# Building a graph's count matrix with ranges of 5 to 13 nodes instead of 25, and spreading the first mean's products

## The chip, the cores and the metric

The kernel runs on 1 core of one Trainium2 chip. The metric is the device time of one execution in microseconds (us), median of the runs shown. An engine works through its own queue in order: TensorE (PE, with its weight loads as PEld), VectorE (DVE), ScalarE (ACT), GpSimd (POOL) and SyncE (SP), which only issues DMAs here. They meet at counting semaphores.

## The reference

Four graph layers, each behind a layer norm and a ReLU, with a residual, on 3125 nodes of 256 features and 50000 edges. `dst` is sorted, and its density falls with the node number as 1/sqrt, so the first nodes have many more edges than the last.

```python
dst = jnp.minimum((3125 * jax.random.uniform(...) ** 2.0).astype(jnp.int32), 99999)   # then sorted
...
edge_index = jnp.stack([src, dst])
h = jnp.maximum(_layernorm(x, axis=-1), 0.0)
x = x + _L0_gnn_ref(h, edge_index, ...)   # hypergraph convolution, twice: mean over dst, then over src
h = jnp.maximum(_layernorm(x, axis=-1), 0.0)
x = x + _L1_gnn_ref(h, ..., src, dst, edge_type_16)      # messages summed by dst, then a GRU cell
h = jnp.maximum(_layernorm(x, axis=-1), 0.0)
x = x + _L2_gnn_ref(h, edge_index, ...)   # GCN
h = jnp.maximum(_layernorm(x, axis=-1), 0.0)
x = x + _L3_gnn_ref(h, edge_index, ...)   # attention
```

## The kernel before

The 3125 nodes are 25 tiles of 125. The kernel first turns the edge list into a dense matrix of edge counts, `adj` (source node by destination node, fp8), with TensorE, in the stage `build`. All layers after it (`main`, from 390 us on) multiply with that matrix. The change lies in `build`, and in two waits of `main`.

In `build` the destination nodes are cut into 125 windows of 25 nodes. A window gets as many **slots** of 128 edges as its expected number of edges asks for, plus a margin: 551 slots in all, from 38 for the first window to 3 for the last. For each slot VectorE writes three one-hot matrices of 128 edges: `hot_lo` (source within its tile, 128 wide, L1516) and `hot_rel` (relation, and destination, L1518), both for eight slots at once in `bulk`, and `hot_keys` (destination within the window times source tile, 625 bytes written as 314 16-bit words, L1528), one instruction for each slot, four to a `quad`. TensorE multiplies them (`window`: L1699 twice per slot, 325 and 300 columns in two PSUM banks, and L1701 once, 25 columns, for the relation counts `CT`). When a window is complete, ScalarE copies both banks into `adj` (`evict`, L1622), and after the fifth window of a tile also `CT` (L1626).

While a tile's windows are built, the product of the tile before it is done: the first mean over `dst`, 25 matmuls of 512 columns (`agg`, L1673), in pieces of 5, 7, 7 and 6 behind the tile's windows. The product of the last tile stands alone at the end. Behind a product come, in turn, `scale_high` on ScalarE (L1632), `combine` on VectorE (L1541), `split` on ScalarE (L1639) and the low half on GpSimd (L1434). The in-degree of a tile is a one-column matmul (`in_degree`, L1680) from `CT`; VectorE reads it in `inverse_degree` (L1534 to L1536).

`hot_lo` and `hot_rel` have two buffers of eight slots: `bulk(m)` waits until TensorE has used the slots of bulk m - 2. `hot_keys` has three buffers of four.

Nothing is scheduled by a planner: the queues are as the code writes them. VectorE's (`vector`) runs through the quads, with the other work put between them: statistics of x after quads 3, 6 and 10, the other groups' keys after quad 8, and `inverse_degree(b - 1)` and `combine(b - 2)` where the last slot of tile b lies.

Ahead of the slots stands a setup chain: a search for the edge number at which each window starts. The last edge of each of 400 chunks is loaded, VectorE counts (L1442), GpSimd gathers one row of 125 for each window (L1417), VectorE counts again, TensorE spreads the windows' starts over the slots (L1713), and GpSimd gathers the edges of all slots in five groups of 128 slots (L1399). Keys are computed (L1463 to L1470), turned by TensorE (L1708), and halved (L1506 to L1510).

Of the kernel before, what the change touches and what calls it, by code (L numbers as in the profile page):

```python
# [24 lines left out]
P = 125  # L25
# [17 lines left out]


def capacities():


    out = []
    for n in range(WINDOWS):
        share = math.sqrt((n + 1) / WINDOWS) - math.sqrt(n / WINDOWS)  # L50
        mean = EDGES * share
        out.append(math.ceil((mean + 5 * math.sqrt(mean * (1 - share))) / SLOT))
    return out


CAP = capacities()
FIRST = [sum(CAP[:n]) for n in range(WINDOWS + 1)]
SLOTS = FIRST[WINDOWS]
GROUPS = -(-SLOTS // SLOT)
PADDED = EDGES + (max(CAP) + 1) * SLOT  # L60
# [66 lines left out]
class Kernel:  # L127


    def __init__(self, nc, ctx, d):  # L130
# [269 lines left out]
def main(k, built):  # L400
# [220 lines left out]
    def tensor(pe):  # L621

        def flip(f):
            i, n = divmod(f, NF)
            if f == 0:
                pe.wait_ge(built["evicted"], WINDOWS)
# [18 lines left out]
        def back1(p):  # L645
# [682 lines left out]
def build(k):  # L1328
# [18 lines left out]
    hot, used, evicted, ct_out = (k.sem("build_" + n) for n in ("hot", "used", "evicted", "ct_out"))  # L1347
    deg_in, deg_out, acc, aw_out, t_ready, hi, lo = (k.sem("build_" + n) for n in ("deg_in", "deg_out", "acc", "aw", "t", "hi", "lo"))

    temp = k.adj_all[:, :, :].rearrange("p t c -> p (t c)").bitcast(F32)  # L1350
    SG = SLOT * GROUPS

    def area(n, width):
        return temp[:, n * SG:n * SG + width]

    raw = temp[:, 0:3 * SG].bitcast(I32).rearrange("p (g e k) -> p g e k", g=GROUPS, k=3)
    raw_rows = temp[:, 0:3 * SG].bitcast(I32).rearrange("p (g n) -> p g n", g=GROUPS)
    tile, lo_key, rel_key, din, hi_key = (area(3 + n, SG).rearrange("p (g e) -> p g e", e=SLOT) for n in range(5))
    win_of, chosen, mark = area(8, SG), area(9, SG), area(10, SG)
    ends, near = area(11, CHUNKS).bitcast(I32), area(12, P).bitcast(I32)  # L1360
    col = area(13, 64)
    pidx, thresh, count, count_i, near_count, before, at2 = (col[:, n:n + 1] for n in (0, 1, 2, 3, 4, 5, 6))
    rhs = col[:, 8:10]
    slot_at, slot_f, slot_i = col[:, 10:10 + GROUPS], col[:, 20:20 + GROUPS], col[:, 30:30 + GROUPS].bitcast(I32)
    where = col[:, 40:40 + 2 * GROUPS].rearrange("p (g k) -> p g k", k=2)
# [1496 lines left out]
```

## Time and profile before

| | |
|---|---|
| median of 3 runs | 1432.39 us (1431.55 to 1432.98) |
| profiled execution | 1432.54 us, its span 1430.5 us |
| PE busy | 1306.7 us (91%), 9866 matmuls |
| DVE busy | 837.4 us (59%) |
| ACT, POOL busy | 437.8 us, 180.2 us |
| `build` | from 0 to 390 us of the span |

Times of rows are microseconds from the span's start, or ns for the mean of one. A matmul's or VectorE instruction's duration overlaps with its neighbour's, so that the rate is read from the distance of the starts.

### The profile page before, as it was taken

How to read it: one execution, taken by the hardware profiler on the slowest of the kernel's cores; microseconds unless marked ns; L12 is line 12 of the kernel's file. 1: busy time of each engine (PE TensorE's matmuls, PEld its weight loads, DVE VectorE, ACT ScalarE, POOL GpSimd, SP SyncE). 2: the span in 40 equal slices, each digit the busy share in tenths (PEclk: the TensorE clock that was granted, in tenths of full speed). 3: DMA queues.
4: the chain of work that ended last, by engine and by line, in shares of the span. 5: the costliest groups of instructions: out<-in, count | busy, mean ns of one | idle time of the engine just before them, and what ended most of it. 6: DMA issues, size and time to landing. Idle time of an engine off the chain costs nothing.

```text
span 1430.5 us, 24598 instructions
## 1 busy us (share of the span) xinstructions
PE 1306.7 (91%) x9866; PEld 1009.1 (71%) x9866; DVE 837.4 (59%) x2257; ACT 437.8 (31%) x971; POOL 180.2 (13%) x321
## 2 busy tenths in 40 slices
PE   2669999999999999999999999999999998999940
PEld 1436666666689999766688888767777777888830
DVE  6999998888545556533335544244535364444566
ACT  3322343444487666211111122122222222222200
POOL 3340000000110000000001111000001011111153
PEclk9779999999999999999999999999999999999975
DMA  5000000000041111200024442011111011111124
GB/s 175 38 20 1 1 1 1 1 1 1 1 158 47 59 47 59 81 1 0 1 82 151 144 157 94 26 34 34 34 34 44 24 34 38 37 36 38 38 62 130
DMA packets 44264, 70.30 MB, mean 49 GB/s; under 512 B 6696, under 2 KB 28551, under 8 KB 44145
## 3 DMA queue, kind: packets, MB, share of 16 engines
q1 hardware_dynamic: 36428, 53.67, 11.2%
q10 hardware_dynamic: 4132, 10.63, 2.2%
q0 software_dynamic: 3584, 4.38, 1.1%
q8 instruction: 79, 1.29, 0.4%
q14 instruction: 41, 0.33, 0.1%
HBM read 38.78 MB, written 29.85 MB: 48 GB/s over the span
## 4 chain that ended last, share of the span: by engine, by line
PE 81%; DVE 12%; POOL 2%; ACT 2%; DMA 1%; issue 1%; POOLq 0%; DVEq 0%; ACTq 0%
PE ps L395 35%; PE ps L675 9%; PE ps L1673 9%; PE ps L1699 7%; PE ps L642 3%; PE ps L736 3%; PE ps L738 3%; DVE big L1528 3%; PE ps L631 2%; POOL adj L618 2%; PE ps L779 2%; PE ps L762 2%; DVE whh L1528 1%; PE ps L742 1%; PE ps L740 1%
## 5 line engine op out<-in xcount | busy, mean ns | idle before, releaser
L395 PE MATMUL ps<-big,pairB 125*128 125x250 fp8e4 (+1 forms) x2600 | 302.9, 267 | 0.6 <-DVE big L1068 0.6
L395 PEld LDWEIGHTS ps<-big,pairB 125*128 125x128 f16 x2600 | 238.8, 98 | 30.0 <-issue 2.8
L590 POOL TENSOR_TENSOR st<-st,mhalf 125x1 f32<-125x1 f32 x100 | 59.3, 593 | 879.0 <-DVE st L1145 879.0
L1622 ACT ACTIVATE adj<-ps 125x325 fp8e4<-125x325 f32 x250 | 99.9, 455 | 199.0 <-PE ps L1701 198.8
L1673 PE MATMUL ps<-pairA,adj 125*125 125x512 f16 x625 | 154.2, 385 | 0.0
L395 PE MATMUL ps<-adj,pairB 125*128 125x250 fp8e4 (+1 forms) x1300 | 146.0, 267 | 1.8 <-DVE pairB L1203 1.8
L395 PE MATMUL ps<-adj,pairA 125*128 125x250 fp8e4 (+1 forms) x1300 | 139.2, 267 | 0.0
L395 PEld LDWEIGHTS ps<-adj,pairB 125*128 125x128 f16 x1300 | 123.2, 98 | 20.0 <-DVE pairB L1203 2.0
L675 PE MATMUL ps<-pairA,adj 125*125 125x512 f16 x625 | 135.2, 379 | 0.0
L395 PEld LDWEIGHTS ps<-adj,pairA 125*128 125x128 f16 x1300 | 120.9, 98 | 19.3 <-issue 7.7
L675 PEld LDWEIGHTS ps<-pairA,adj 125*125 125x125 fp8e4 x625 | 85.7, 137 | 48.9
L1528 DVE TENSOR_SCALAR big<-big 128x314 uint16<-128x314 f16 x368 | 114.8, 381 | 0.0
L1673 PEld LDWEIGHTS ps<-pairA,adj 125*125 125x125 fp8e4 x625 | 77.8, 137 | 36.7
L1701 PE MATMUL ps<-wih 128*128 128x25 bf16 x551 | 98.2, 178 | 0.0
L1174 DVE TENSOR_TENSOR big<-ps,gates_b 125x512 f32<-125x512 f32 x25 | 17.2, 688 | 117.8 <-PE ps L742 117.8
L1068 DVE CAST big<-ps 125x500 fp8e4<-125x500 f32 (+1 forms) x87 | 53.8, 625 | 51.4 <-PE ps L631 51.1
L1699 PE MATMUL ps<-big,W 128*128 128x325 fp8e4 x376 | 67.7, 310 | 14.9 <-DVE big L1528 14.7
L885 ACT ACTIVATE whh<-adj 125x1625 fp8e4<-125x1625 fp8e4 (+1 forms) x50 | 75.1, 1501 | 0.1
L1701 PEld LDWEIGHTS ps<-wih 128*128 128x128 bf16 x551 | 56.2, 102 | 26.4
L1699 PE MATMUL ps<-big,Wg 128*128 128x325 fp8e4 x360 | 63.1, 303 | 4.4 <-DVE big L1528 4.3
L631 PE MATMUL ps<-identb,adj 125*125 125x125 bf16 x625 | 63.3, 222 | 3.4 <-ACT big L878 3.3
L1528 DVE TENSOR_SCALAR whh<-big 128x314 uint16<-128x314 f16 x184 | 60.4, 393 | 4.0 <-PE ps L1701 4.0
(239 smaller groups left out, 1772.8 us busy)
## 6 DMA issues: line engine op xcount, KB each, us to landing
t_adjTp<-big SPq DMA_DIRECT2D x25, 400.0 KB, 2.3
big<-t_adjTp ACTq DMA_DIRECT2D x25, 400.0 KB, 3.9
t_xh<-work SPq DMA_DIRECT2D x13, 256.0 KB
t_z<-big SPq DMA_DIRECT2D x25, 128.9 KB
pairB<-in_x SPq DMA_DIRECT2D x5, 640.0 KB, 11.6
t_h0p<-pairB SPq DMA_DIRECT2D x5, 640.0 KB
work<-t_xh SPq DMA_DIRECT2D x25, 128.0 KB, 2.3
xin<-t_xh SPq DMA_DIRECT2D x25, 128.0 KB, 2.3
```

The costliest lines, as they stand in the source:

```text
L395: last = pe.matmul(out, src[:, j, FEAT * part + 128 * c:FEAT * part + 128 * (c + 1)], rhs(j, p), start=(j + part == 0 and not begun), stop ...
L590: g.tensor_tensor(st[:, 9:10], st[:, 8:9], k.mhalf[:, 0:1], ALU.pow).then_inc(S[rstd], 1)
L631: last = pe.matmul(k.ps[0:P, f % 4, (j - j0) * P:(j - j0 + 1) * P], k.adj[:, i, PITCH * j:PITCH * j + P], k.identb[:, 0:P], start=True, st ...
L642: last = pe.matmul(k.ps[0:P, 6 + i % 2, 0:FEAT], stationary(i // 2 % 2, i, c), w[:, c, :], start=(c == 0), stop=(c == KC - 1))
L675: last = pe.matmul(k.ps[0:P, i % 4, :], k.adj[:, j, PITCH * i:PITCH * i + P], k.pairA[:, j, :], start=(j == 0), stop=(j == TILES - 1))
L885: s.activation(junk[:, 0:(j1 - j0) * P].rearrange("p (j c) -> p j c", c=P), cols[:, i, j0:j1, 0:P], ACT.Copy, saturate=False, accum_out=(k ...
L1068: v.tensor_copy(slots[:, i % 4, j0:j1, 0:P], k.ps[0:P, f % 4, 0:(j1 - j0) * P].rearrange("p (j c) -> p j c", c=P), saturate=False).then_in ...
L1528: last = v.tensor_scalar(k.hot_keys[q % 3][:, u, 0:HALVES * 2].bitcast(U16), k.iota_keys[:, 0:HALVES], k.key_half[:, s:s + 1], k.key_byte[ ...
L1622: last = s.activation(out[:, :, d0:d1], k.ps[0:P, 2 * (n % 2) + a, 0:(d1 - d0) * TILES] .rearrange("p (n j) -> p j n", j=TILES), ACT.Copy, ...
L1673: last = pe.matmul(k.ps[0:P, 6 + i % 2, :], k.adj[:, j, PITCH * i:PITCH * i + P], k.pairA[:, j, :], start=(j == 0), stop=(j == TILES - 1))
L1699: pe.matmul(k.ps[0:128, bank + a, 0:(d1 - d0) * TILES], low, keys[:, d0 * TILES:d1 * TILES], start=start, stop=True, skip_group_check=True)
L1701: pe.matmul(k.ps[0:128, 4 + b % 2, WIN * q:WIN * (q + 1)], rel[:, 0:128], rel[:, 128:128 + WIN], start=start, stop=True, skip_group_check= ...
```

## The change

- The windows are narrower, and their width differs from tile to tile (5 to 13 nodes, `tile_windows`): 405 windows and 606 slots. By tile, from the first: 102, 49, 40, 32, 28, 25, 25, 21, 20, three of 21, three of 18, four of 16, five of 14, and 13 slots. A slot is one key matmul of 125 to 325 columns and one relation matmul of 5 to 13 columns; L1528's successor writes 63 to 163 words.
- Neighbouring windows of a tile share a PSUM bank up to 20 nodes (197 **blocks**), and four banks are in turn. ScalarE empties a block at a time.
- `hot_keys` has a ring of 32 slots and no wait of its own; `hot_lo` and `hot_rel` keep two buffers of eight. `bulk` now writes the keys too.
- The 25 matmuls of a tile's product are given out slot by slot by a list, `SUMMED`: in even steps over the slots from number 104, but not before five slots after the tile's last. Evaluated, the list spreads the product of tile 0 over slots 107 to 124; all 25 of each product of tiles 1 to 21 stand behind one slot, the fifth after the tile's last (156, 196, 228, 256, 281, 306, 327, 347, 368, 389, 410, 428, 446, 464, 480, 496, 512, 528, 542, 556, 570).
- ScalarE reads the in-degree (`degree`); VectorE's `inverse_degree(t)` comes after the bulk with slot END[t] - 2, and `combine(t)` after the bulk with slot END[t] + 14, where END[t] is the slot behind which the product of tile t ends.
- The setup searches each slot's window directly: GpSimd writes a table of the first node of each slot's window with 36 runs, each an iota for the node and most a second for the slots to skip; TensorE turns it into columns; five gathers of chunk rows take the place of one.
- `main` waits for all 25 low halves ahead of its first product, where it waited for 22 and then for each of the last.

In VectorE's queue, one tile late in the build (`W`, `Wg` are `hot_lo`, `wih` is `hot_rel`, `big` and `whh` hold `hot_keys`). Before:

```order
L1516 TENSOR_TENSOR W<-big,work 128x1024 [waits build_used]
L1518 TENSOR_TENSOR wih<-big,work 128x8x2x25
L1528 TENSOR_SCALAR whh<-big 128x314 [waits build_used]
L1528 TENSOR_SCALAR whh<-big 128x314 x3
L1534 COPY indeg<-ps 125x1 [waits build_deg_in]
L1535 TENSOR_SCALAR rsB<-ps 125x1
L1536 RECIPROCAL rsB<-rsB 125x1 [waits build_ok]
L1541 SCALAR_TENSOR_TENSOR work<-ps,rsB,work 125x256 [waits build_lo,build_aw]
L1528 TENSOR_SCALAR big<-big 128x314 [waits build_used]
L1528 TENSOR_SCALAR big<-big 128x314 x3
```

And now, the bulks of slots 464 to 471 and 472 to 479 and what follows them (slot 474 is the last of tile 15):

```order
L1607 TENSOR_TENSOR W<-big,work 128x1024 [waits build_used]
L1609 TENSOR_TENSOR wih<-big,work 128x8x2x16
L1618 TENSOR_SCALAR whh<-big 128x100 x8
L1607 TENSOR_TENSOR Wg<-big,work 128x1024 [waits build_used]
L1609 TENSOR_TENSOR wih<-big,work 128x8x2x16
L1618 TENSOR_SCALAR whh<-big 128x100 x2
L1618 TENSOR_SCALAR whh<-big 128x63
L1618 TENSOR_SCALAR whh<-big 128x100 x5
L1633 SCALAR_TENSOR_TENSOR work<-ps,rsB,work 125x256 [waits build_lo,build_aw]
L1626 TENSOR_SCALAR rsB<-indeg 125x1 [waits build_deg_out]
L1627 RECIPROCAL rsB<-rsB 125x1 [waits build_ok]
L1607 TENSOR_TENSOR W<-big,work 128x1024 [waits build_used]
```

Before, the degree read here was that of a tile whose slots had been past for a tile; now it is that of the tile whose last slot is five slots back, and it stands ahead of the next bulk. In TensorE's queue late in the build, before:

```order
L1680 MATMUL ps<-ones,CT 125x1 [waits build_ct_out]
L1673 MATMUL ps<-pairA,adj 125x512 [waits build_t,build_evicted]
L1673 MATMUL ps<-pairA,adj 125x512 x4
L1699 MATMUL ps<-big,W 128x325 [waits build_hot,build_evicted]
L1699 MATMUL ps<-big,W 128x300
L1701 MATMUL ps<-wih 128x25
```

And now, at slots 511 and 512:

```order
L1767 MATMUL ps<-ones,CT 125x1 [waits build_ct_out]
L1783 MATMUL ps<-whh,Wg 128x200 [waits build_evicted]
L1785 MATMUL ps<-wih 128x8
L1783 MATMUL ps<-big,W 128x200 [waits build_hot]
L1785 MATMUL ps<-wih 128x8
L1760 MATMUL ps<-pairA,adj 125x512 [waits build_t]
L1760 MATMUL ps<-pairA,adj 125x512 x24
L1783 MATMUL ps<-big,W 128x200 [waits build_evicted]
```

The one-column matmul of the degree now stands just ahead of a slot that waits for VectorE (`build_hot`), and the product is in one piece behind that slot. In GpSimd's queue, from the first gather on, before:

```order
L1417 DMA adj<-in_dst_rows,adj 125x125 [waits build_first]
L1389 IOTA big 128x640
L1420 MEMSET ones 128x125
L1394 TENSOR_TENSOR work<-work,mhalf 125x5 [waits build_var]
L1396 TENSOR_TENSOR work<-work 125x5 [waits build_rstd]
L1399 DMA adj<-in_edges,adj 128x384 [waits build_indexed]
L1399 DMA adj<-in_edges,adj 128x384 x4
```

And now:

```order
L1467 DMA adj<-in_dst_rows,adj 128x125 [waits build_chunk]
L1451 TENSOR_TENSOR work<-work,mhalf 125x5 [waits build_var]
L1453 TENSOR_TENSOR work<-work 125x5 [waits build_rstd]
L1467 DMA adj<-in_dst_rows,adj 128x125 [waits build_chunk] x2
L1472 DMA adj<-in_edges,adj 128x384 [waits build_indexed]
L1467 DMA adj<-in_dst_rows,adj 128x125 [waits build_chunk] x2
L1472 DMA adj<-in_edges,adj 128x384 [waits build_indexed] x4
```

Three more instructions and a wait (`build_var`) stand between the first row gather and the first gather of edges; ahead of it stand 56 iotas instead of 16. The core of the diff:

```diff
+def tile_windows(tile):
+    best = None
+    for width in range(5, WIDEST + 1):
+        cuts = [(a, min(a + width, P)) for a in range(0, P, width)]
+        need = [slots_for(P * tile + a, P * tile + b) for a, b in cuts]
+        cost = sum(n * (33 + b - a) for n, (a, b) in zip(need, cuts))
+        if best is None or cost < best[0]:
+            best = cost, cuts, need
+    return best[1:]
...
+    cost = [33 + WINDOWS[w].width for w in SLOT_WINDOW]
+    total, past, done, out = sum(cost[SUM_FROM:]), 0, 0, []
+    for s in range(SLOTS):
+        if s >= SUM_FROM:
+            past += cost[s]
+            ready = TILES * sum(stop + 5 <= s for stop in STOP)
+            done = max(done, min(ready, round((TILES - 1) * TILES * past / total)))
+        out.append(done)
...
@@ main, tensor
-                if p == 0 and c == 0 and (j == 0 or j >= EARLY):
-                    pe.wait_ge(built["lo"], max(j + 1, EARLY))
+                if p == 0 and u == 0:
+                    pe.wait_ge(built["lo"], TILES)
@@ build, vector
-        def quad(q):
-            if q >= 3:
-                dve.wait_ge(used, QUAD * (q - 2))
-            for u in range(QUAD):
-                s = QUAD * q + u
-                last = v.tensor_scalar(k.hot_keys[q % 3][:, u, 0:HALVES * 2].bitcast(U16), k.iota_keys[:, 0:HALVES],
+            for u in range(BULK):
+                s = BULK * m + u
+                if s >= SLOTS:
+                    break
+                n = (TILES * WINDOWS[SLOT_WINDOW[s]].width + 1) // 2
+                last = v.tensor_scalar(k.hot_keys[m % RING][:, u, 0:2 * n].bitcast(U16), k.iota_keys[:, 0:n],
                                        k.key_half[:, s:s + 1], k.key_byte[:, s:s + 1], ALU.is_equal, ALU.mult)
+                if u % QUAD == QUAD - 1 or s == SLOTS - 1:
+                    last.then_inc(hot, 1)
...
+            for t in range(TILES):
+                if (END[t] - 2) // BULK == m:
+                    inverse_degree(t)
+                if (END[t] + 14) // BULK == m:
+                    combine(t)
@@ build, scalar
+            act.wait_ge(used, blk.stop)
+            s.activation(k.adj[:, :, PITCH * i + blk.at:PITCH * i + blk.at + blk.width], k.ps[0:P, n % 4, 0:blk.width * TILES]
+                         .rearrange("p (n j) -> p j n", j=TILES), ACT.Copy, scale=1.0 / CNT, saturate=False).then_inc(evicted, 1)
...
+        for m in range(SLOTS + 64):
+            while counted < TILES and STOP[counted] + 6 <= m:
+                degree(counted)
...
+            while n < len(BLOCKS) and BLOCKS[n].stop <= m:
+                evict(n)
...
+            while halved < TILES and END[halved] + 16 <= m and halved < scaled:
+                split(halved)
...
+            while scaled < TILES and END[scaled] + 2 <= m:
+                scale_high(scaled)
@@ build, tensor
+        for s in range(SLOTS):
+            if STOP[counted] + 4 == s:
+                in_degree(counted)
+                counted += 1
...
+            slot(s)
+            while done < SUMMED[s]:
+                t, j = divmod(done, TILES)
+                agg(t, j, j + 1)
+                done += 1
```

## Rows read from the trace of the kernel before

**Rows 1.** The page: TensorE's granted clock in 40 slices of the span.
```profile
PEclk9779999999999999999999999999999999999975
```
**Rows 2.** Timeline of the setup (start, duration, engine, line, what, idle before).
```profile
1.76 2.85 POOL L1389 IOTA adj<- 128x38 f32 x12
...
7.56 1.36 POOL L1417 DMA_INDIRECT adj<-in_dst_rows,adj  x1 [2.73 <-DVE adj L1555]
...
9.68 1.74 DVE L1448 BATCH_NORM_STATS2 work<-pairB 125x6 f32<-125x256 f32 x5 [1.07 <-DMA pairB<-in_x]
...
12.26 1.21 POOL L1394 TENSOR_TENSOR work<-work,mhalf 125x5 f32<-125x5 f32 x1 [2.47 <-DVE work L1454]
...
14.69 0.15 DVE L1562 COPY adj<-adj 125x1 f32<-125x1 f32 x1 [2.52 <-DMA adj<-in_dst_rows,adj]
...
18.96 1.24 POOL L1399 DMA_INDIRECT adj<-in_edges,adj  x1 [5.22 <-DVE adj L1571]
...
24.51 0.24 DVE L1463 CAST adj<-adj 128x128 f32<-128x128 int32 x1
...
28.53 0.23 DVE L1506 TENSOR_SCALAR big<-work 128x128 f32<-128x128 f32 x1 [1.89 <-ACT work L1615]
...
29.90 1.23 DVE L1516 TENSOR_TENSOR W<-big,work 128x1024 bf16<-128x1024 f16 x1
```
**Rows 3.** DMA issues, 0 to 60 us: KB each, us from issue to landing.
```profile
adj<-in_edges,adj POOLq DMA_INDIRECT x5, 3.8
```
**Rows 4.** Timeline of VectorE, one bulk of eight slots and the next.
```profile
87.79 1.21 DVE L1516 TENSOR_TENSOR Wg<-big,work 128x1024 bf16<-128x1024 f16 x1
88.92 0.57 DVE L1518 TENSOR_TENSOR wih<-big,work 128x400 bf16<-128x400 f16 x1
89.41 2.26 DVE L1528 TENSOR_SCALAR big<-big 128x314 uint16<-128x314 f16 x8
91.58 1.22 DVE L1516 TENSOR_TENSOR W<-big,work 128x1024 bf16<-128x1024 f16 x1
```
**Rows 5.** Groups of VectorE by form (busy us, mean ns | idle before).
```profile
L1557 DVE TENSOR_SCALAR adj<-adj 125x640 f32<-125x640 f32 x1 | 0.5, 544 | 0.0
L1467 DVE TENSOR_SCALAR adj<-adj 128x512 f32<-128x512 f32 x1 | 0.4, 427 | 0.0
L1467 DVE TENSOR_SCALAR adj<-adj 128x128 f32<-128x128 f32 x1 | 0.2, 227 | 0.0
```
**Rows 6.** Timeline of TensorE, two slots at the full clock.
```profile
92.08 0.43 PE L1699 MATMUL ps<-big,Wg 128*128 128x325 fp8e4 x2
92.34 0.17 PE L1701 MATMUL ps<-wih 128*128 128x25 bf16 x1
92.37 0.43 PE L1699 MATMUL ps<-big,Wg 128*128 128x325 fp8e4 x2
```
**Rows 7.** Timeline of TensorE: end of tile 0's product, and the last ones.
```profile
120.40 1.49 PE L1673 MATMUL ps<-pairA,adj 125*125 125x512 f16 x6
...
365.51 1.29 PE L1673 MATMUL ps<-pairA,adj 125*125 125x512 f16 x5
...
375.87 1.29 PE L1673 MATMUL ps<-pairA,adj 125*125 125x512 f16 x5
...
384.46 5.61 PE L1673 MATMUL ps<-pairA,adj 125*125 125x512 f16 x25
```
**Rows 8.** Timeline: an eviction of ScalarE, and what follows the last product.
```profile
287.32 0.75 ACT L1622 ACTIVATE adj<-ps 125x325 fp8e4<-125x325 f32 x2 [1.35 <-PE ps L1701]
...
390.11 0.47 ACT L1632 ACTIVATE work<-ps,rsB 125x256 f32<-125x256 f32 x1 [4.41 <-PE ps L1673]
...
390.62 0.48 DVE L1541 SCALAR_TENSOR_TENSOR work<-ps,rsB,work 125x256 f32<-125x256 f32 x1 [5.03 <-ACT work L1632]
```
**Rows 9.** Busy time by stretch: PE, PEld, DVE, ACT, POOL, granted clock, DMA, GB/s.
```profile
48.00:50.00 2.00, 0.01 (x1) 0.00 (x0) 1.93 (x13) 0.00 (x0) 1.05 (x1) 1.00 0.79 328
50.00:52.00 2.00, 1.99 (x12) 1.19 (x12) 2.00 (x4) 0.00 (x0) 1.55 (x2) 0.56 0.00 0
```

More of the change, by code:

```diff
@@ L42 @@
 BATCH = 5
[L45 to L52, printed above, removed]
-    return out
[L56 to L60, printed above, removed]
+ORDER = tuple(range(TILES))
+Window = namedtuple("Window", "turn at width slots slot block")
@@ new lines, with summing @@
+WINDOWS, BLOCKS, RUNS = plan()
+SLOTS = sum(w.slots for w in WINDOWS)
+SLOT_WINDOW = [n for n, w in enumerate(WINDOWS) for _ in range(w.slots)]
+GROUPS = -(-SLOTS // SLOT)
+RUN_SPLIT = next(r[0] for r in RUNS if r[0] >= SLOT)
+PADDED = EDGES + (max(w.slots for w in WINDOWS) + 1) * SLOT
+def summing():
+    cost = [33 + WINDOWS[w].width for w in SLOT_WINDOW]
[6 more added lines that the diff above has]
+        out.append(done)
+    return out
@@ L1357, in build @@
[L1357 to L1363, printed above, removed]
@@ L1364, in build, with part_row @@
-    slot_at, slot_f, slot_i = col[:, 10:10 + GROUPS], col[:, 20:20 + GROUPS], col[:, 30:30 + GROUPS].bitcast(I32)
-    where = col[:, 40:40 + 2 * GROUPS].rearrange("p (g k) -> p g k", k=2)
+    def part_row(row, count, at, width):
+        return k.adj_all[:, row:row + count, SPARE + 4 * at:SPARE + 4 * (at + width)].bitcast(F32)
+    raw_rows = part_row(0, GROUPS, 0, 3 * SLOT).bitcast(I32)
+    raw = raw_rows.rearrange("p g (e k) -> p g e k", k=3)
+    tile, lo_key, rel_key = (part_row(5, GROUPS, SLOT * n, SLOT) for n in range(3))
@@ new lines, in build @@
+    din, hi_key = (part_row(10, GROUPS, SLOT * n, SLOT) for n in range(2))
+    ends = part_row(15, 1, 0, CHUNKS).rearrange("p o c -> p (o c)").bitcast(I32)
+    near = part_row(16, GROUPS, 0, P).bitcast(I32)
+    mark = part_row(16, GROUPS, P + 3, CHUNKS // 2).bitcast(F16)
+    col = part_row(22, 1, 0, 128).rearrange("p o c -> p (o c)")
+    pidx = col[:, 0:1]
+    where = col[:, 10:10 + 2 * GROUPS].rearrange("p (g k) -> p g k", k=2)
+    count, near_count, slot_f = (col[:, 20 + 10 * n:20 + 10 * n + GROUPS] for n in range(3))
@@ L1423, in gpsimd @@
-        for n in range(GROUPS):
+        table(RUN_SPLIT, SLOTS)
+        iota(k.iota_keys, [[1, KWI]], 0, 0)
+        g.memset(k.ho_all[:, :], 0.0).then_inc(iotas, 1)
+        gather_near(0)
+        root(0)
+        gather_near(1)
+        gather_near(2)
+        gather(0)
+        for n in range(3, GROUPS):
+            gather_near(n)
+        for n in range(1, GROUPS):
             gather(n)
@@ new lines, in inverse_degree, with combine @@
+        def inverse_degree(t):
+            i = ORDER[t]
+            dve.wait_ge(deg_out, t + 1)
+            own.link(v.tensor_scalar(k.rsB[:, i:i + 1], k.indeg[:, i:i + 1], 1.0, 1.0 / CNT, ALU.max, ALU.mult))
+            v.reciprocal(k.rsB[:, i:i + 1], k.rsB[:, i:i + 1]).then_inc(known, 1)
+        def combine(t):
+            i = ORDER[t]
+            dve.wait_ge(aw_out, t + 1)
+            wait_past(dve, lo, t - 1)
+            stt(out=k.t[t % 2], in0=k.ps[0:P, 6 + t % 2, FEAT:2 * FEAT], scalar=k.rsB[:, i:i + 1], in1=k.aw[t % 2],
@@ L1572, in vector @@
+        starts(0, 1)
+        moments_of(0)
+        keys(0, 1)
+        starts(1, GROUPS)
         magnitudes()
```

377 lines of the change are left out of this document (193 added, 184 removed).

## The prediction

> **What bounds the kernel now.** I read the clock and the busy shares by slices first: after the first twelfth of the span TensorE is busy and at its full clock throughout [rows 1], so nothing later than the build can hide or give anything. The build is the only stage changed. Its timelines show three parts. Until 29.90 us a chain over all engines finds the edges of the slots; the first bulk of one-hot matrices starts there [rows 2]. From there to tile 0's product, which ends at 120.40 + 1.49 = 121.9, VectorE never rests: eight slots cost it 91.58 - 87.79 = 3.79 us [rows 4], and TensorE only about 0.29 us a slot [rows 6], 2.3 us for eight. From then on TensorE sets the pace: a late tile takes 375.87 - 365.51 = 10.36 us [rows 7], which is 15 slots of 0.29 (4.4) and 25 products in 5.61 [rows 7]. The last product ends at 390.1. What follows is the same in both kernels, so I forecast the place of that end. The new wait for all low halves in the main stage costs nothing: the last low half follows its product by about 2.5 us (two of its steps take 1 us, [rows 8]), and in both kernels 14 groups of transposes stand between.
>
> **The new prices.** TensorE: eight VectorE-made slots showed 92.37 - 92.08 = 0.29 us for 650 columns; 650 columns at 2.4 GHz are 0.27, so a slot of 26 x width columns costs (26 x width)/2400 + 0.02: 0.10 for width 7, 0.11 for 8. VectorE: `hot_lo` keeps 88.92 - 87.79 = 1.13 us for eight slots; `hot_rel` goes from 400 to 256 elements, 0.49 to 0.33. A key instruction of 314 words took 2.17/8 = 0.27 [rows 4]. Its size now falls to 63 to 163 words, and the trace has no such size. The 640-wide one took 544 ns, and 384 elements more cost 427 - 227 = 200 ns without a column operand [rows 5]: 1.95 elements per ns. Taking size off, the 640-wide one has 544 - 328 = 216 ns left, and the key instruction, whose duration is 2.26 - 7 x 0.272 = 0.358 us [rows 4], has 358 - 161 = 197: nearly the same fixed part, so I take two elements a cycle for it too, and for the distance of two of them 0.272 - 0.161, 0.11 us, + words/1950. The bounds are this and all of it fixed (0.27). Width 7 gives 0.154, width 8 0.160, so a slot costs VectorE 0.18 + 0.16 = 0.34 us instead of 0.47.
>
> The Trainium skill ("VectorE: DVE Perf Modes", the perf-mode tier table) has `tensor_scalar` on 16-bit data in SBUF at four elements a cycle, not two. By that rule the 314-wide instruction is 0.19 fixed and 0.08 by size, and the narrow ones would be 0.05 to 0.06 dearer than I take. The equal fixed parts above speak for two; what four would give is a rival below.
>
> **Setup.** GpSimd has 53 table iotas where 12 took 2.85 us [rows 2]: between 0.11 (the short ones lie that close) and 0.24 each, 6 to 13 us, so the first row gather issues at 9 to 15 instead of 7.56. Its rows landed at 14.69, 7.1 us on, while the loads of x filled the queues; the edge gathers needed 3.8 [rows 3]. I take 15. Then, one behind another: count and start of group 0, 1.3 (16.3); the statistics of x, 9.68 to 12.26, 2.6 (18.9); `root`, 1.4 (20.3), which now stands ahead of the edges' gather in GpSimd's queue; two row gathers, 2.6 (22.9); the edges' own gather 3.8 (26.7); keys 2.2 (28.9); the other four groups' starts 2.4 (31.3); what stood between 18.6 and 24.51 [rows 2], 5.9 (37.2); halves 29.90 - 28.53 = 1.4. The first bulk starts at 38.7: **+8.8 us** (+4 if only the last links count, +15 with the dear iotas).
>
> **To the end of tile 0's product.** Before: 121.9 - 29.9 = 92.0 us, of which 130 slots of 3.79/8 are 61.6; the rest, 30.4, is statistics, keys and VectorE's slow stretch beside GpSimd, and stays, less the second halves (2.2), which come at slot 128. Now the product ends behind slot 124: 15.5 bulks of 1.46 + 8 x 0.154 = 2.70 are 41.9, with 28.2 it is 70.1: **-21.9**.
>
> **From there to the last product.** Before 390.1 - 121.9 = 268.2 us. Engine by engine the new work is far less. A tile of 16 slots is 16 x 0.11 + 5.6 = 7.4 us of TensorE and 16 x 0.34 + 0.9 = 6.4 of VectorE. But the rows of the order show them taking turns. VectorE may stand at most two bulks ahead of TensorE, and after the bulk that holds slot END - 2 it waits in `inverse_degree` for a matmul that TensorE reaches only after the previous product and nearly a whole tile of slots. Where END is the first slot of a bulk (or the second), the product stands behind a slot of the bulk that VectorE starts after that wait. Nine tiles are such: those ending at 256, 281, 368, 464, 480, 496, 512, 528 and 584. One round of the 16-slot ones, from a product's end:
> - ScalarE: `scale_high` 0.5 [rows 8]; seven evictions, each 0.75/2 [rows 8] + 75 more columns, 0.45: 3.1; CT, split and degree 0.9: **4.5**. The slots of TensorE hide under these.
> - VectorE: degree to reciprocal 0.5, then 1.46 + 4 x 0.16 until four slots are ready: **2.7**.
> - TensorE: the slot and 25 products: **5.7**.
>
> Together 13.0, where a tile took 10.36. Seven of the nine are like it: 91. The one of 28 slots has two more bulks to make, 16.0; the one of 25 one small bulk more, 13.2: 120.2 in all. In the other tiles the product starts within a bulk that is made, VectorE gets 9 to 16 slots ahead under it, and the round is 5.6 + 1.4 (scale, combine) + 1.2 (degree) + the slots that are left at 0.34, and not under 9.0, ScalarE's pace. Tiles 1 to 3 (49, 40, 32 slots): 18.0, 17.9, 15.4. The eleven others: 12.1, 11.1, 9.7, 10.2, 11.8, 9.9, 10.6, 9.0, 9.9, 9.2, 9.9, that is 113.4. The last product follows its neighbour by 6.5. Sum 51.3 + 120.2 + 113.4 + 6.5 = 291.4: **+23.2**.
>
> **The clock.** TensorE now rests about 3 us ahead of each of the nine products and works little in the slots before. In the trace such a rest (0.01 us busy in 48 to 50) was followed by a granted 0.56, the 1.2 GHz level in most of the stretch [rows 9]. A product that starts there for 3.5 us loses 1.75. None of 25 would be 0, all 44. I take half of the nine: **+8**.
>
> **Sum.** 8.8 - 21.9 + 23.2 + 8 = +18. The profiled execution took 1432.54 (span 1430.5), the median is 1432.39, so 1432.5 + 18 = **1450 us**.
>
> **The rivals.**
> - *Every product starts at the low clock*: 10 + 44 = +54, 1486 us. For it: in the tiles bound by VectorE, too, TensorE works 0.8 us of 2.7. Against: the clock is back within the product each time.
> - *A narrow key instruction is mostly fixed cost.* At four elements a cycle the 0.272 of 314 words is 0.19 fixed and 0.08 by size; at the mean of 98 words that is 0.216 instead of 0.159, 0.057 more per slot: 7 us in the 124 slots before the first product, 7 in the first six tiles outside the products, 5 in the quads waited for: +19, 1469 us. Against it stands the fixed part of [rows 5]. (This is where the Trainium skill's tier table, named above, would lead.)
> - *The turns overlap* (faster). The place is `inverse_degree`, the price ScalarE's 4.5 us. If TensorE reaches the degree's matmul 2.6 us sooner, twenty tiles gain 2 us each: 1432.5 + 10 - 40 = 1402; with no turns at all the sum of each tile's dearer engine is 211 instead of 291, 1362 us. It decides from an average round of 11.7 us instead of 12.1 (and no clock loss) towards faster. Against it stand the two queues; for it, that my 4.5 us is a sum of neighbours that may lie closer.
> - *No change*: the setup is hidden (the starts of the other groups need not be waited for long) and the clock stays: 1434, within 0.2% (about what a measurement of this kernel can tell from no change).
>
> **Chances and range.** Forecast 0.57, dear key instructions 0.12, low clock 0.12, overlap 0.14, no change 0.05. Slower is 0.57 + 0.12 + 0.12 = 0.81, faster 0.14, same 0.05. The forecast's own range is 1436 to 1468 (setup +4 to +15, clock 0 to 16, ScalarE's part 3.9 to 5). The range that leaves out two in ten reaches to no change below and to the middle of the low-clock case above: 1430 to 1480.
>
> **What would show it.** The first bulk near 39 us; eight narrow key instructions 1.23 to 1.28 us apart; tile 0's product ending near 109; late rounds of about 13 us at the nine places and 9 to 10 elsewhere, with VectorE idle ahead of the degree's instruction and TensorE ahead of the slot of END; the last product near 400 to 410. Rounds of 8 to 9 us at tiles 14 to 18 would make the forecast wrong; so would a first bulk at 31.

## The result and the profile after

The changed kernel takes 1498.6 us (median of 4 runs, 1497.49 to 1500.08), the kernel before 1432.7 (1431.55 to 1434.64): ratio 1.0459, 95% interval 1.0441 to 1.0477. It is slower by 66 us. Forecast were 18, and the range ended at 1480. The last product of `build` ends at 455.33 us of the span instead of 390.07 [rows 7]: 65.3 of the 66 us lie ahead of it, as the prediction said that all of it would. Behind it 1040.6 us follow, and before the change 1040.4.

| | forecast | measured |
|---|---|---|
| first bulk starts (before 29.90) | 38.7 | 42.31 |
| tile 0's product ends (before 121.89) | 108.8 | 121.06 |
| from there to the last product's end (before 268.2) | 291.4, and 8 for the clock | 334.3 |
| last product ends (before 390.07) | 400 to 410 | 455.33 |

The page of the changed kernel, its shares and its granted clock by slices, to be held against [rows 1]:

```profile
span 1495.9 us, 23712 instructions
...
PE 1263.2 (84%) x9435; PEld 979.7 (65%) x9435; DVE 821.0 (55%) x2318; ACT 431.8 (29%) x943; POOL 195.8 (13%) x365
...
PE   1246768676888999999999999999999998999940
...
DVE  4998766764554555653333555333544545544576
...
PEclk9557678888899999999999999999999999999975
```

A slice is 37.4 us, so the slots are built from slice 2 to the beginning of slice 13. In slices 3 to 12 TensorE is busy for 40 to 80%, and in slices 2 to 11 its granted clock is 0.5 to 0.8. VectorE is full only in slices 2 and 3 and falls to 40 or 50% by slice 10. Two engines that both rest in one stage wait for each other, or for a third.

Setup, the timeline of GpSimd and VectorE (start, duration, line, in brackets the idle time before and what ended it), which answers to [rows 2]:

```profile
1.64 2.52 POOL L1446 IOTA CT<- 1x21 f32 x18
...
4.48 6.97 POOL L1446 IOTA CT<- 1x2 f32 x35
...
12.35 1.13 POOL L1467 DMA_INDIRECT adj<-in_dst_rows,adj  x1 [0.19 <-issue]
...
18.35 1.15 DVE L1643 MEMSET big<- 32x1312 uint32 x1 [0.33 <-issue]
...
19.96 0.34 DVE L1512 TENSOR_SCALAR_CACHE_REDUCE adj<-adj 128x125 f16<-128x125 int32 x1
...
27.83 0.95 POOL L1472 DMA_INDIRECT adj<-in_edges,adj  x1 [0.30 <-issue]
...
30.87 0.46 DVE L1554 CAST adj<-adj 128x128 f32<-128x128 int32 x1 [7.40 <-DMA adj<-in_edges,adj]
...
42.31 1.23 DVE L1607 TENSOR_TENSOR W<-big,work 128x1024 bf16<-128x1024 f16 x1
...
43.45 0.42 DVE L1609 TENSOR_TENSOR wih<-big,work 128x256 bf16<-128x256 f16 x1
...
43.79 1.79 DVE L1618 TENSOR_SCALAR big<-big 128x88 uint16<-128x88 f16 x8
...
45.48 1.22 DVE L1607 TENSOR_TENSOR Wg<-big,work 128x1024 bf16<-128x1024 f16 x1
```

Eight key instructions of 88 words lie 45.48 - 43.79 = 1.69 us, 0.211 each, where 0.154 was forecast; a bulk is 45.48 - 42.31 = 3.17 us, not 2.70. The wide ones of 314 words lay 0.272 apart [rows 4].

One late round, of 16 slots, on ScalarE, VectorE and TensorE (the same view). Product 14 ends at 339.23. What to see is the baton: ScalarE empties banks and splits first and reads the degree only at 342.71, VectorE has waited for it, TensorE waits for VectorE's key matrix, and the product of this tile stands behind that slot.

```profile
339.27 0.47 ACT L1711 ACTIVATE work<-ps,rsB 125x256 f32<-125x256 f32 x1 [7.53 <-PE ps L1760]
...
339.64 2.01 ACT L1696 ACTIVATE adj<-ps 125x400 fp8e4<-125x400 f32 x5
...
341.50 0.23 ACT L1699 COPY CT<-ps 16x125 f32<-16x125 f32 x1
...
341.78 0.37 PE L1767 MATMUL ps<-ones,CT 16*125 16x1 f32 x2 [0.43 <-ACT CT L1699]
...
342.71 0.14 ACT L1704 COPY indeg<-ps 125x1 f32<-125x1 f32 x1
...
342.89 0.15 DVE L1626 TENSOR_SCALAR rsB<-indeg 125x1 f32<-125x1 f32 x1 [2.63 <-ACT indeg L1704]
...
343.16 1.47 DVE L1607 TENSOR_TENSOR W<-big,work 128x1024 bf16<-128x1024 f16 x1
...
344.89 1.80 DVE L1618 TENSOR_SCALAR big<-big 128x100 uint16<-128x100 f16 x8
345.89 0.35 PE L1783 MATMUL ps<-big,W 128*128 128x200 fp8e4 x1 [3.53 <-DVE big L1618]
...
346.10 7.49 PE L1760 MATMUL ps<-pairA,adj 125*125 125x512 f16 x25
...
346.61 1.22 DVE L1607 TENSOR_TENSOR Wg<-big,work 128x1024 bf16<-128x1024 f16 x1
```

ScalarE's part is 342.89 - 339.23 = 3.7 us, forecast 4.5; VectorE's is 345.89 - 342.89 = 3.0, forecast 2.7. Together 6.7, forecast 7.2. Then slot and product take 7.7 instead of 5.7: behind the rest the 25 matmuls last 7.49 us, where they last 5.59 at the full clock. The round is 14.4 us, forecast 13.0.

The waits of the stage by line (us in total, times, longest), from 42 to 456 us:

```profile
PE ps L1783 <- DVE whh L1618: 63.2, 31, 6.3
...
PE ps L1783 <- DVE big L1618: 57.3, 31, 6.1
DVE work L1633 <- ACT work L1711: 49.8, 11, 5.9
...
DVE rsB L1626 <- ACT indeg L1704: 30.5, 20, 6.2
```

TensorE waits 120.5 us for key matrices, while VectorE waits 80.3 us for ScalarE, which waits for TensorE's products. Of the 120.5 us, 40.3 lie ahead of the end of tile 0's product, where VectorE set the pace before, too. The other 80.2 lie in the rounds behind it (from 121.1 to 456 us):

```profile
PE ps L1783 <- DVE whh L1618: 44.9, 25, 3.6
PE ps L1783 <- DVE big L1618: 35.3, 21, 3.5
```

Before, the rounds (from 121.9 to 390 us) had 1.2 us of such waits:

```profile
PE ps L1699 <- DVE big L1528: 0.7, 2, 0.5
PE ps L1699 <- DVE whh L1528: 0.5, 1, 0.5
```

The clock of three stretches (the columns are those of [rows 9]):

```profile
60.00:80.00 20.00, 6.57 (x48) 5.10 (x48) 19.76 (x39) 11.79 (x29) 17.58 (x21) 0.58 0.22 85
100.00:120.00 20.00, 14.62 (x111) 10.33 (x112) 18.63 (x63) 3.13 (x8) 0.00 (x0) 0.64 0.00 1
340.00:360.00 20.00, 12.01 (x77) 7.49 (x75) 10.42 (x32) 6.94 (x22) 1.33 (x2) 0.83 0.00 0
```

In the first TensorE is busy for 6.57 of 20 us and granted 0.58, that is the 1.2 GHz level for most of the time; in the third both levels alternate within a round (0.50 from 346 to 350 us, in the product shown above, and 1.00 from 350 to 353.6).

### The profile page after: what moved, and what is told of

It is laid out like the page before. It is cut to its first block, busy times and chain, and to the rows that moved or that the text cites. A ratio compares the mean times of both kernels' runs of the same rounds, so it can differ in the third digit from the quotient of the medians.

```text
span 1495.9 us, 23712 instructions
## 1 busy us (share of the span) xinstructions
PE 1263.2 (84%) x9435; PEld 979.7 (65%) x9435; DVE 821.0 (55%) x2318; ACT 431.8 (29%) x943; POOL 195.8 (13%) x365
## 4 chain that ended last, share of the span: by engine, by line
PE 69%; DVE 7%; ACT 3%; POOL 2%; issue 2%; DMA 0%; POOLq 0%; DVEq 0%; ACTq 0%
PE ps L449 34%; PE ps L729 9%; PE ps L1760 8%; PE ps L696 3%; PE ps L790 3%; PE ps L792 3%; PE ps L685 2%; POOL adj L672 2%; PE ps L833 1%; PE ps L816 1%; PE ps L794 1%; PE ps L796 1%; ACT adj L1696 1%; PE ps L762 1%; DVE whh L1618 1%
## 5 line engine op out<-in xcount | busy, mean ns | idle before, releaser
L1760 PE MATMUL ps<-pairA,adj 125*125 125x512 f16 x625 | 176.8, 445 | 0.0
L1760 PEld LDWEIGHTS ps<-pairA,adj 125*125 125x125 fp8e4 x625 | 98.8, 163 | 61.3 <-issue 29.3
L729 PE MATMUL ps<-pairA,adj 125*125 125x512 f16 x625 | 135.2, 379 | 0.0
L1696 ACT ACTIVATE adj<-ps 125x450 fp8e4<-125x450 f32 (+7 forms) x197 | 89.5, 511 | 115.1 <-PE ps L1785 114.8
L729 PEld LDWEIGHTS ps<-pairA,adj 125*125 125x125 fp8e4 x625 | 85.5, 137 | 49.1
L1785 PE MATMUL ps<-wih 128*128 128x7 bf16 (+7 forms) x606 | 90.1, 183 | 0.0
L1228 DVE TENSOR_TENSOR big<-ps,gates_b 125x512 f32<-125x512 f32 x25 | 17.2, 688 | 117.9 <-PE ps L796 117.9
L1618 DVE TENSOR_SCALAR whh<-big 128x88 uint16<-128x88 f16 (+7 forms) x302 | 74.8, 353 | 0.0
L1618 DVE TENSOR_SCALAR big<-big 128x88 uint16<-128x88 f16 (+7 forms) x304 | 74.3, 325 | 0.0
L1504 POOL TENSOR_TENSOR pairB<-work,pairB 125x256 f16<-125x256 f32 x25 | 22.7, 909 | 346.5 <-ACT pairB L1719 346.5
L1785 PEld LDWEIGHTS ps<-wih 128*128 128x128 bf16 x606 | 60.4, 100 | 6.0 <-issue 0.5
L932 ACT ACTIVATE big<-ps 125x500 fp8e4<-125x500 f32 (+1 forms) x88 | 47.3, 541 | 46.4 <-PE ps L685 46.4
```

Of the source, the lines that this page charges most:

```text
L729: last = pe.matmul(k.ps[0:P, i % 4, :], k.adj[:, j, PITCH * i:PITCH * i + P], k.pairA[:, j, :], start=(j == 0), stop=(j == TILES - 1))
L932: s.activation(slots[:, i % 4, j0:j1, 0:P], k.ps[0:P, f % 4, 0:(j1 - j0) * P].rearrange("p (j c) -> p j c", c=P), ACT.Copy, saturate=False ...
L1618: last = v.tensor_scalar(k.hot_keys[m % RING][:, u, 0:2 * n].bitcast(U16), k.iota_keys[:, 0:n], k.key_half[:, s:s + 1], k.key_byte[:, s:s ...
L1696: s.activation(k.adj[:, :, PITCH * i + blk.at:PITCH * i + blk.at + blk.width], k.ps[0:P, n % 4, 0:blk.width * TILES] .rearrange("p (n j) - ...
L1760: last = pe.matmul(k.ps[0:P, 6 + t % 2, :], k.adj[:, j, PITCH * i:PITCH * i + P], k.pairA[:, j, :], start=(j == 0), stop=(j == TILES - 1))
L1785: pe.matmul(k.ps[0:128, 4 + blk.turn % 2, win.at:win.at + win.width], rel[:, 0:128], rel[:, 128:128 + win.width], start=start, stop=True, ...
```

## The experiments

Theory A: TensorE, VectorE and ScalarE take turns at `inverse_degree` and `combine`; dear key instructions and TensorE's low clock make each turn longer. Theory B: the clock alone makes the extra time. Theory C: VectorE's work bounds the rounds. All ran with the kernel before on the same chip (its medians 1433.2 to 1434.0 us). Where an expectation gives a number of the changed kernel, it is 1498.6. The changed kernel itself was not run again beside them, and the kernel before was 0.6 to 1.3 us above the 1432.7 of the result, so that a difference of one or two us from 1498.6 says nothing.

**Fillers for the clock, everywhere.**

```diff
+            fill = 0
+            if s >= 112 and s == win.slot:
+                fill = win.slots + (16 if s // BULK != WINDOWS[SLOT_WINDOW[s - 1]].slot // BULK else 0)
+            for _ in range(fill):
+                pe.matmul(k.ps[0:P, 4 + blk.turn % 2, 258:512], k.pairA[:, 0, 0:P], k.pairA[:, 1, 0:254], ...)
```

> The changed kernel with extra 254-column matmuls on TensorE that nothing reads (into the unused part of the relation bank), 16 about each bulk's first slot and one for each slot from slot 112 on, so that it hardly rests; no queue is reordered. Theory A (engines take turns; the rests lower the clock; a narrow key instruction is 0.21 us): all products at 5.6 us, which gives back up to 33 us of the 66, rounds of about 13 us stay at the nine places; 1465 to 1480 us. Theory B (the low clock alone is what is lost, the order of the queues is harmless): 1430 to 1445 us. Theory C (VectorE's work is the bound): no change, 1495 to 1500.

Measured: 1547.97 us, ratio to before 1.0799 (1.0781 to 1.0817), a miss. The products of tiles 1 to 21 came back to 5.59 us and the clock of the run is 0.971, but the fillers took 220.9 us of TensorE. The group of them, from 42 to 503 us (busy us, mean ns of one), and one of their long rows on TensorE's timeline:

```profile
L1781 PE MATMUL ps<-pairA 125*125 125x254 f16 x1485 | 220.9, 279 | 0.0
...
386.79 2.04 PE L1781 MATMUL ps<-pairA 125*125 125x254 f16 x17
```

In a row they lie (2.04 - 0.30)/16 = 0.109 us apart at the full clock (the last lasts 0.30). The mean of 220.9/1485 = 0.149 is higher because about a third of them stand singly or in pairs between slots, where one keeps TensorE busy for 0.27 to 0.30 us. Four 16-slot rounds became 14.8 to 15.0 us, with TensorE's own fillers in them. Every theory's range lies below the result. So the clock follows TensorE's work, but the price of the clock can't be read from this run.

**The degree one bulk later.**

```diff
-                if (END[t] - 2) // BULK == m:
+                if (END[t] + 6) // BULK == m:
...
-            if (END[t] - 2) // BULK > m:
+            if (END[t] + 6) // BULK > m:
```

> The changed kernel with inverse_degree(t) put after the bulk that holds slot END + 6 instead of END - 2, nothing else. Theory A: VectorE no longer waits for a matmul behind a whole tile of TensorE's slots; the rounds at the nine places fall from 14.4 to about 9 or 10 us, and fewer products start at the low clock: 40 to 50 us less, 1445 to 1460 us. Theory B: the rests move but remain, within 8 us of 1498.6. Theory C: no change.

Measured: 1470.62 us, ratio 1.0254 (1.0236 to 1.0271): 28 us less than the changed kernel for moving a two-instruction step. The clear part of A holds: no work is gone, so C can't explain it. Nor can B, which allowed 8 us: the products' busy time fell by 6.3 us (176.8 to 170.5). The rounds of tiles 15 to 18 fell from 14.4, 14.0, 13.8 and 15.5 us to 9.1, 10.8, 10.8 and 9.2. Two products of it, on TensorE's timeline:

```profile
303.63 7.12 PE L1760 MATMUL ps<-pairA,adj 125*125 125x512 f16 x25
...
315.11 5.59 PE L1760 MATMUL ps<-pairA,adj 125*125 125x512 f16 x25
```

Nearly all of the gain lies at the nine places, 139.0 to 111.8 us together. It is below the 40 to 50 us expected, because tiles 9 and 14 still take 15.5 and 13.9 us (14.9 and 16.3 without the edit) and tiles 1 to 6 nearly kept their rounds (21.8, 22.8, 18.5, 18.8, 14.7, 16.5 against 21.6, 22.7, 18.4, 19.8, 16.7, 16.6): it is not the degree that holds them. The changed kernel's rows ahead of the product of tile 2 show what does, two waits of several for keys, one for each bulk:

```profile
152.51 0.33 PE L1783 MATMUL ps<-whh,Wg 128*128 128x175 fp8e4 x1 [1.47 <-DVE whh L1618]
155.69 0.35 PE L1783 MATMUL ps<-big,W 128*128 128x200 fp8e4 x1 [1.50 <-DVE big L1618]
157.28 8.03 PE L1760 MATMUL ps<-pairA,adj 125*125 125x512 f16 x25
```

TensorE uses each bulk as VectorE makes it, 3.18 us apart, and the product comes on top, at a low clock. VectorE can't use that time fully, since `hot_lo` and `hot_rel` have two buffers: in this run it waits 47.0 us in the rounds for TensorE to use slots. No run with more buffers was made.

**Each product spread over the next tile's slots.**

```diff
-            ready = TILES * sum(stop + 5 <= s for stop in STOP)
-            done = max(done, min(ready, round((TILES - 1) * TILES * past / total)))
+            for t in range(TILES - 1):
+                a, b = STOP[t] + 5, STOP[t + 1] + 5
+                if a <= s < b:
+                    done = max(done, TILES * t + round(TILES * (s - a + 1) / (b - a)))
```

> The changed kernel with a list that really spreads each product evenly over the slots from five after its tile's end to five after the next tile's end (END and the places of degree and combine follow from it). Theory A: no pieces of 25 products, no turns, full clock; VectorE's 606 slots of 0.39 us set the build: about 100 us less than the changed kernel, 1395 to 1410 us, faster than before. Theory B: full clock gives 33 us back, 1460 to 1470. Theory C: no change.

Measured: 1399.96 us, ratio 0.9764 (0.9747 to 0.978), inside A's 1395 to 1410: 98.6 us less than the changed kernel and 34 less than before, with the same instructions. Their order is another on TensorE, and since END follows the list, the degree, `scale_high`, `combine` and `split` of a tile come later on VectorE and ScalarE, too; the edit doesn't part the two, and the next experiment shows only that a later degree adds nothing to it. The windows of 60 us late in its `build`:

```profile
260.00:320.00 60.00, 60.00 (x435) 39.56 (x434) 56.13 (x174) 35.90 (x89) 9.42 (x7) 1.00 0.00 1
```

TensorE is busy for all of it at the full clock, and VectorE for 56.13 of 60. The rounds from tile 11 on are 8.0 to 8.3 us instead of 8.5 to 16.3; nobody passes a baton, since TensorE always has matmuls of the previous product between two slots. VectorE's 80.3 us of waiting for ScalarE become 8.4. Of TensorE's 120.5 us of waiting for keys 58.3 are left, 44.4 of them until the end of tile 0's product (133.47 now) and none behind tile 10:

```profile
PE ps L1785 <- DVE big L1620: 31.4, 21, 6.1
PE ps L1785 <- DVE whh L1620: 26.9, 17, 5.7
```

**Both of these edits.**

> The spread list and the late degree together. Theory A: within 5 us of the spread list alone, since END already lies a tile later there. Theory B and C: as with the spread list alone.

Measured: 1400.53 us, ratio 0.9764. With the products spread the later degree is worth nothing: the two edits remove the same wait.

**Eleven fillers at each bulk only.** As the first experiment, with `fill = 11` at the first window of a new bulk, and 0 elsewhere.

> The changed kernel, with 11 extra matmuls of 254 columns at the first window that reads each new bulk from slot 112 on (into a corner of a bank that is cleared afterwards), none elsewhere. In the filled run before this one such a matmul cost 0.147 us, so a bulk's cost is 11 x 0.147 = 1.6 us. Theory A (three causes: taking turns, a low clock in the products, dear keys): the products after tile 2 come back from 6.7-8.5 us to about 5.6, which is up to 30 us; the fillers stand partly in the rests and cost 0 to 60 x 1.6 = 90 us where they don't. If the rests of TensorE cover them, 1467-1480; if they don't, 1500-1530, and then the sum of the products' excess over 5.6 is still near 0 and the granted clock near 0.97. Theory B (the clock alone made the extra time): rounds fall to those of the kernel before, 1430-1440 or less. Theory C (VectorE's work bounds the rounds): no change of the rounds, 1495-1502, whatever the clock.

Measured: 1498.07 us, ratio 1.0446 (1.043 to 1.0462), the changed kernel's time to within 0.5 us, though the granted clock of the run rose from 0.918 to 0.968, and that of the build from 0.77 to 0.95. It lies between A's two ranges, and 58 us above B's. C's range, 1495 to 1502, holds it: this run alone can't tell A from C, and it is the later degree above and the fewer keys below that speak against C. A's condition was met by half: at seven of the nine places the product still took 7.2 to 8.5 us, and of the 33 us by which the products exceed 5.6 each 16 are left. TensorE from the first bulk to the last product, in the changed kernel and in the filled one (busy time by engine, the columns of [rows 9]):

```profile
42.31:455.33 413.02, 283.81 (x1906) 189.77 (x1907) 293.80 (x881) 129.01 (x342) 51.79 (x55) 0.77 0.02 7
```

```profile
42.31:456.92 414.61, 331.04 (x2588) 253.48 (x2589) 294.54 (x883) 131.01 (x342) 48.44 (x56) 0.95 0.02 7
```

The products of the changed kernel, then products and fillers of the filled one with its waits for keys:

```profile
L1760 PE MATMUL ps<-pairA,adj 125*125 125x512 f16 x625 | 176.8, 445 | 0.0
```

```profile
L1760 PE MATMUL ps<-pairA,adj 125*125 125x512 f16 x625 | 161.3, 415 | 0.0
L1781 PE MATMUL ps<-pairA 125*125 125x254 f16 x682 | 87.9, 279 | 0.0
```

```profile
PE ps L1789 <- DVE whh L1618: 41.0, 22, 6.3
PE ps L1789 <- DVE big L1618: 34.3, 19, 6.1
```

The fillers take 87.9 us, but TensorE is busy for only 47.2 more: the rest of its work takes 40.7 us less. Of these, 31 lie in the groups of products (15.5), key matmuls (9.7) and relation matmuls (5.5), and the other 10 were not taken apart. TensorE's idle time falls by 45.6 us, from 129.2 to 83.6, nearly all of it waits for keys (120.5 to 75.3). Together 86.3 for 87.9. A clock bought with dummy work was worth what it cost.

**Fewer key instructions.**

```diff
+                if u % QUAD == 1 and s < SLOTS - 1:
+                    if m < RING:
+                        v.memset(k.hot_keys[m][:, u, :].bitcast(U16), 0)
+                    continue
```

> The changed kernel without the key instruction of two of every eight slots (their pairs are left out of the counts, so the matrix is not complete); in the first four bulks a clear stands in its place. A bulk then costs VectorE 0.84 us more for the comparisons plus 6 x 0.211 = 1.27, in all 2.75 against 3.17, which is about what the prediction had charged for a whole bulk (2.70). It prices the key term of the sum. Theory A: of the turns' rounds each of some 33 slow rounds has one to two bulks in line, so 0.42 to 0.84 us each, and tiles before product 0 take about 14 bulks x 0.42 = 6 us: 1476-1486, with the clock still low in the products. Theory B (clock alone): 1495-1500. Theory C (VectorE's work bounds): the work falls by 152 x 0.211 = 32 us and the time by all of it, 1464-1470.

It leaves the pairs of two slots in eight out of the counts; TensorE still multiplies all slots. Measured: 1479.48 us, ratio 1.032 (1.0304 to 1.0336), 19.1 us less, inside A's 1476 to 1486, above C's 1464 to 1470 and below B's 1495. Tile 0's product ends at 114.25 instead of 121.06 (6.8 us), the rounds take 320.8 instead of 334.3 (13.5 us). Of the 32 us of work that were taken from VectorE, 13 made no difference, since it waits for others meanwhile.

**The start of the edges' gather.** On the kernel with spread products:

```diff
         gather_near(0)
+        gather(0)
         root(0)
-        gather_near(1)
-        gather_near(2)
-        gather(0)
-        for n in range(3, GROUPS):
+        for n in range(1, GROUPS):
             gather_near(n)
```

and in VectorE's queue `starts(1, GROUPS)` stands behind bulk 0.

> The kernel with spread products (1400.0 us), with the order of GpSimd's work at the start changed alone: the two gathers of group 0 go ahead of the other groups' near gathers, and the starts of groups 1 and later are worked out by VectorE after bulk 0 instead of ahead of it. Setup theory (the first bulk is late by GpSimd's and VectorE's waiting line, not by the transfers themselves): the first bulk falls from 42.3 to 35-37 us and the time by as much, 1392-1395. Rival (the rows of the first edges land no earlier, since the queue shares them): first bulk and time unchanged within 1 us, 1399-1401. Second rival (the other groups come late and stall bulks 8 and later): 1400-1410.

Measured: 1393.44 us, ratio 0.9718 (0.9705 to 0.9731), 6.5 us less than without the edit, a time inside the 1392 to 1395 expected. The edges' gather issues at 21.35, 6.5 us sooner than in the changed kernel, and the first bulk starts at 33.72, 8.6 us sooner (35 to 37 was expected):

```profile
21.35 0.97 POOL L1474 DMA_INDIRECT adj<-in_edges,adj  x1 [7.86 <-DVE adj L1545]
...
24.45 0.24 DVE L1554 CAST adj<-adj 128x128 f32<-128x128 int32 x1 [0.99 <-DMA adj<-in_edges,adj]
...
33.72 1.23 DVE L1607 TENSOR_TENSOR W<-big,work 128x1024 bf16<-128x1024 f16 x1
```

The transfer takes 3.1 us whether it starts here or at 27.83, so those 6.5 us were the waiting line on GpSimd: `root` waits for VectorE's statistics, and the gather stood behind it. The other 2.1 us are `starts` on VectorE, which now stands behind bulk 0: it was moved to where VectorE sets the pace, and `build` ends only 6.7 us sooner (349.88 against 356.56).

**Wider ranges.** On the kernel with spread products:

```diff
-WIDEST = 13
-KW, KWI = 328, 164
+WIDEST = 15
+KW, KWI = 376, 188
...
-        cost = sum(n * (33 + b - a) for n, (a, b) in zip(need, cuts))
+        cost = sum(n * (60 + b - a) for n, (a, b) in zip(need, cuts))
```

> The kernel with spread products (1400.0 us), with ranges of up to 15 nodes (keys up to 376 wide instead of 328) and a slot priced in the choice of ranges at 60 + width instead of 33 + width: about 575 slots instead of 606. Theory A (the key instruction is mostly a fixed cost and the matmul of a slot too, so slots count more than words): 31 slots fewer x (0.211 key + 0.10 of the bulk's comparisons) = 10 us of VectorE, and TensorE's slots lose 31 x 0.137 less what the wider ones add: 1388-1393. Rival (each key pays for its width; the change's balance was right): 1399-1404.

Measured: 1398.15 us (1396.65 to 1398.72), ratio 0.9747 (0.9734 to 0.9761), 1.8 us less than with the products spread alone: a miss for A's 1388 to 1393, and just below the rival's 1399. The intervals of the two ratios overlap, so that the gain is not clear of noise. There are 580 slots, but the 580 key instructions together took 148.8 us of VectorE and the 606 took 149.3: the wider ones ate what the fewer ones gave. Width still has a price, which the expectation had left out on VectorE.

**Start and ranges together.**

> The two edits of the last pair together on the kernel with spread products (1400.0 us): the order of GpSimd's work at the start (measured -6.5 us alone) and ranges of up to 15 nodes (measured -1.8 us alone). If the two are independent, 1391-1392 us; the rival (the ranges' gain lay in the stretch before product 0, where the earlier start already gives it) says 1393-1394.

Measured: 1390.98 us (1389.56 to 1391.81), ratio 0.9704 (0.9691 to 0.9717). That is what adding the two gives (1391.6), and below the rival's 1393; against the start alone, whose interval overlaps with this one, the step is small. This is the fastest version found: 42 us, 3.0%, below the kernel before, and 108 us below the changed one. Its late stretch is bound by TensorE at the full clock:

```profile
240.00:320.00 80.00, 80.00 (x581) 52.67 (x580) 71.93 (x226) 48.34 (x118) 7.52 (x10) 1.00 0.00 1
```

## Why the prediction was right and wrong

*Sign, place, mechanism: right.* The chance of 0.81 was on slower; all of the loss lies in `build`; and the taking of turns is shown: two edits that take no work away, the later degree and the spread products, give 28 and 99 us. The order showed it before any trace of the changed kernel did. The late round fits step by step up to the slot (6.7 us against 7.2). The nine places take 139.0 us against 120.2, and 121.6 without the 17.4 that the low clock costs their products. What failed are the sizes of two terms, the clock and the key instruction, and with them the range, which ended at 1480.

*The clock: the step that failed most.* "I take half of the nine: +8." Beyond 5.6 us each, products 1 to 24 take 33 us together (176.8 of busy time less 24 x 5.6, less 9.4 of product 0, which has slots between its matmuls). 1 us of it is product 23, which ran at the full clock with slots between its matmuls; the other 32 are the low clock: **+24** over the term. All nine places pay, 17.4 us, where the argument let half of them pay. Eight products that it left out, those of tiles 1 to 3, 6, 8, 11, 12 and 21, pay 14.5. The argument counted the rests ahead of the nine. But the clock was low before the first product was due (0.58 in 60 to 80, 0.64 in 100 to 120), and the first six, which VectorE holds up, take 6.7 to 8.2 us. The rival "every product cold" (+44) was nearer. Its evidence stood in the prediction itself: VectorE-bound, TensorE works 0.8 us of 2.7. What the clock costs in the end stays partly open, and the sum below takes the 32 in full: the filled run gave 41 us of TensorE's time back and needed as much for it, and no run raised the clock without giving TensorE other matmuls.

*The key instruction: wrong.* "So I take two elements a cycle for it too": 0.154 us forecast, 0.211 measured. Between 314 words (0.272, [rows 4]) and 88 (0.211) 226 words cost 0.061 us, 3.7 a nanosecond, and 0.19 us don't depend on size. The four elements a cycle of the Trainium skill ("VectorE: DVE Perf Modes", the perf-mode tier table), from which the prediction had worked out 0.19 fixed, agree with this trace; the equal "fixed parts" of [rows 5] came from an instruction without column operands and from one duration, and the likeness was chance. The run with fewer key instructions, whose bulks cost about what the prediction charged, prices it: **+6.8** ahead of product 0 and **+13.5** in the rounds, where the sum had nothing for it. The rival had said +19 in all.

*Setup: right in mechanism, 3.6 us short.* The iotas cost 0.14 and 0.20 each, within the bounds, and the row gather issued at 12.35, within the 9 to 15. The step that failed is "I take 15" for its rows. They landed at 17.2, 4.9 us behind the issue, and VectorE took them up only at 19.96: from 15.12 on its queue had the counts of the other groups and two clears ahead of them, for which the prediction had no term. From there on the links fit: the edges' gather issued at 27.83, forecast 22.9, and the first bulk followed 14.5 us behind, forecast 15.8.

*Closing the sum.* 1450 + 3.6 (setup) + 8.7 (slots to product 0: 78.8 us against 70.1; 6.8 of it dear keys, 1.9 not explained) + 24 (clock) + 13.5 (keys in rounds) = 1499.8. The turns proper were forecast at 291.4, and 334.3 - 32 - 13.5 leaves 288.8 for them, 2.6 less. That gives 1497.2; the profiled execution took 1497.6, and the median is 1498.6. Two rivals that were priced one at a time came true in large part together, on top of the forecast, while the range was drawn as if only one could. That the turns come out within 1% is partly luck: single rounds, with the low clock taken off, lie from 1.2 us below their forecast (tile 22) to 2.4 above it (tile 2).

*What wasn't weighed.* That the products could stand elsewhere. The prediction had the engine sums, "far less" than the forecast: 70.1 + 211 = 281 us from the first bulk to the last product, where it forecast 361.5 and 8 for the clock. The spread kernel takes 314.3 (42.24 to 356.56), and the changed one 413.0. With the products spread, the rest of the change is worth 34 us; the list that placed them turned that into a loss.

## What to carry to other kernels

When a change makes both engines' work smaller but places one long burst (here 25 matmuls) behind a slot that waits for the other engine, write down who hands the baton to whom for one round before adding up work; then spread the burst so that each engine always has something in its queue. Rivals that share a cause, like rests of TensorE, its clock, and a dearer producer ahead of it, add up: a range should hold their sum. A price for a new size of an instruction is read from two sizes of the same instruction or left between its bounds, not completed by likeness to another form.

## What the runs showed of the hardware

- A `tensor_scalar` with two column operands, from 16-bit to 16-bit data, was 0.211 us from its neighbour at 88 words, and 0.215 at 100 ((346.61 - 344.89)/8).
- Matmuls of 254 columns, weights loaded for each, lay (2.04 - 0.30)/16 = 0.109 us apart in a row at the full clock. Over a whole run they took 0.129 us of TensorE's busy time each with 11 at a bulk (682 in 87.9 us) and 0.149 with a third of them between slots (1485 in 220.9).
- Short iotas of two elements lay 6.97/35 = 0.20 us apart, those of 21 elements 2.52/18 = 0.14.
- TensorE's granted clock rose from 0.918 to 0.968 over the run with 11 more matmuls at each bulk, and the time stayed. Of the changed kernel's own four runs, the two at 0.939 took 1499.6 and 1500.1 us, the two at 0.917 and 0.918 took 1497.5 and 1497.6.
